# Routed rows scattered into one DRAM region per expert, tiles loaded plainly and turned on VectorE

## What is computed

```python
x = x + xattn(ctx_512, layernorm(x), Wq, Wk, gamma_raw)      # top-30% mask of similarities, made symmetric
h = layernorm(x).reshape(-1, 512)                            # 2048 tokens
scores = sigmoid(h @ router_w)                               # 2048 x 32
# 4 of 8 groups by their best two, then the best 8 experts in them
top_k_index = top_k(masked(scores + router_bias), 8)
tkw = 2.5 * scores[top_k_index] / sum(scores[top_k_index])
xs = repeat(h, 8)[argsort(top_k_index)]                      # 16384 rows, sorted by expert
down = ragged_dot(silu(ragged_dot(xs, w_gate)) * ragged_dot(xs, w_up), w_down)   # 512 -> 256 -> 512
shared = silu(h @ sw_gate) * (h @ sw_up) @ sw_down           # 512 -> 512 -> 512
x = x + sum_of_8(down * tkw) + shared
```

## Time and profile before

| | |
|---|---|
| median of 3 runs | 1012.5 us |
| profiled execution | 1009.42 us |
| its span, first to last instruction | 1007.7 us |
| PE (TensorE) busy | 905.1 us, 90% |
| DVE (VectorE) busy | 576.2 us, 57% |
| ACT (ScalarE) busy | 501.0 us, 50% |
| POOL (GpSimd) busy | 448.7 us, 45% |
| first matmul of the first expert tile | at 311.61 us |
| row transposes (L1490) | 592, on 148 tiles |

### The profile page before, as it was taken

The page is one execution under the profiler, slowest core; times in us unless marked ns, Lnnn a source line. Parts: engine busy times, 40 slices in busy tenths (PEclk is TensorE's granted clock), DMA queues, the critical chain, the costliest instruction groups (busy, mean ns, idle before and its releaser), DMA issues.

```text
span 1007.7 us, 21989 instructions
## 1 busy us (share of the span) xinstructions
PE 905.1 (90%) x4596; PEld 489.2 (49%) x4597; DVE 576.2 (57%) x1285; ACT 501.0 (50%) x994; POOL 448.7 (45%) x348
## 2 busy tenths in 40 slices
PE   4358798897969999999999999999999999999994
PEld 1143354544534555555555555555555555555542
DVE  5868798897886443446353455444455555463321
ACT  4376482752224444456454464545556455464331
POOL 1131011110033566555656665646465564566653
PEclk8569878898879999999999999999999999999998
DMA  4122021111228678878878888887788888787864
GB/s 155 42 80 80 1 85 54 43 46 42 93 84 270 155 177 191 184 170 222 185 168 192 180 186 196 169 221 171 175 219 204 234 187 235 174 187 127 147 114 77
DMA packets 90268, 149.25 MB, mean 148 GB/s; under 512 B 9649, under 2 KB 46769, under 8 KB 90225
## 3 DMA queue, kind: packets, MB, share of 16 engines
q0 software_dynamic: 33120, 80.64, 40.3%
q1 hardware_dynamic: 57104, 68.13, 21.2%
HBM read 101.55 MB, written 47.20 MB: 148 GB/s over the span
## 4 chain that ended last, share of the span: by engine, by line
PE 58%; issue 4%; DVE 3%; ACTq 2%; ACT 2%; DVEq 2%; POOL 0%; POOLq 0%
PE bank L258 49%; PE bank L1490 5%; PE bank L1481 3%; ACTq L1158 1%; ACT gu L240 1%; DVEq L1158 1%; DVE hid L1391 1%; DVE gu L247 1%; DVE mark_p L400 0%; DVE mark_q L407 0%; DVE dn L250 0%; ACTq L240 0%; DVEq L247 0%; DVE hid L309 0%; POOL out_dram L1201 0%
## 5 line engine op out<-in xcount | busy, mean ns | idle before, releaser
L258 PE MATMUL bank<-gu,xgT 128*128 x1764 | 404.8, 379 | 1.4 <-issue 1.4
L1201 POOL DMA_INDIRECT out_dram<-y,ids_i x145 | 236.4, 1630 | 233.3 <-DMA out_dram<-y,ids_i 120.5
L1383 DVE TENSOR_TENSOR xgT<-bank,xgT 128x512 f16<-128x512 f32 x148 | 102.2, 691 | 283.2 <-ACT xgT L1244 233.8
L258 PEld LDWEIGHTS bank<-gu,xgT 128*128 128x128 f16 x1764 | 172.4, 98 | 176.9 <-issue 1.6
L258 PE MATMUL bank<-dn,hT 128*128 x870 | 211.7, 379 | 0.8
L1189 POOL DMA_INDIRECT xg<-xrows,ids_i x153 | 167.0, 1092 | 68.3 <-issue 42.4
L1244 ACT CAST xgT<-bank 128x512 f16<-128x512 f32 x148 | 86.9, 588 | 135.6 <-issue 128.5
L1269 ACT ACTIVATE y<-bank 128x512 f32<-128x512 f32 x145 | 87.2, 601 | 110.1 <-PE bank L258 93.0
L258 PEld LDWEIGHTS bank<-dn,hT 128*128 128x128 f16 x870 | 84.9, 98 | 75.3 <-issue 7.8
L1250 ACT ACTIVATE silu<-bank 128x256 f32<-128x256 f32 x147 | 56.1, 382 | 97.7 <-PE bank L258 85.4
L1391 DVE SCALAR_TENSOR_TENSOR hid<-bank,xg,silu 128x256 f32<-128x256 f32 x147 | 70.6, 480 | 59.1 <-ACT silu L1250 52.7
(11 more groups left out here) (217 smaller groups left out, 793.4 us busy)
## 6 DMA issues: line engine op xcount, KB each, us to landing
stage_gu<-in_L_ffn_w_gate_dram SPq DMA_DIRECT2D x32, 512.0 KB
stage_gu<-in_L_ffn_w_up_dram SPq DMA_DIRECT2D x32, 512.0 KB
stage_dn<-in_L_ffn_w_down_dram SPq DMA_DIRECT2D x32, 512.0 KB
x_sb<-in_x_dram SPq DMA_DIRECT2D x4, 1024.0 KB, 6.7
xrows<-adj SPq DMA_DIRECT2D x4, 1024.0 KB, 4.2
out_dram<-acc SPq DMA_DIRECT2D x4, 1024.0 KB, 4.6
xg<-xrows,ids_i POOLq DMA_INDIRECT x153
out_dram<-y,ids_i POOLq DMA_INDIRECT x145
```

The source lines that it names most:

```text
L258: last = nc.tensor.matmul(out_ap, stationary(a, c), moving(w, c), start=(c == 0 and (a, w) == parts[0]), stop=(c == chunks - 1 and (a, w) ...
L1201: g_.indirect_dma_start(out, bass.IndirectOffsetOnAxis(ap=ids_i[:, t:t + 1], axis=0), y[:, t % YS, :], None, compute_op=ALU.add).then_inc( ...
L1383: v.tensor_tensor(xgT[:, s, 1, :, :], bank[XB[s]][:, :].rearrange("p (k t) -> p k t", k=KC), xgT[:, s, 0, :, :], ALU.subtract).then_inc(S[ ...
```

## The change

`xrows` and its gather are gone. A DRAM tensor `places` holds for each expert 16 x 128 row places, and 32 tiles more for rows that don't count. At routing each row goes to the place that its slot names: one indirect DMA for 128 tokens and one of their 8 choices (`dispatch_rows`), 32 for a batch and 128 in all, on GpSimd's queue. 24 of a batch stand in the first block in the pass behind its keys, 8 in the next pass between `s_low` 1 and 2; of batch 2 the last 8, and all 32 of batch 3, stand in the second block. The rest of each expert's last tile is filled with zeros by one more such DMA per expert (`fill_up`). Tiles are then read by SP with plain loads, five per tile (`load_rows`): four 128-column pieces, each onto 32 partitions in runs of 512 bytes, and the shares in runs of 128 bytes. VectorE turns a tile in 32x32 blocks with one instruction (`turn_rows`), whose result has the order of hidden values p * 4 + k; the weights of gate and up are loaded in the same order, which gives runs of 4 KB. SP's loop now goes over tiles. The row splits read SBUF instead of PSUM. `acc` and `xT16` keep fewer batches.

```diff
+        places = nc.dram_tensor("places", [E * TT + E, P, HR], F32).ap()
...
+        def dispatch_rows(pool, b, n):
+
+            k, i = TOP_EXPERTS - 1 - n // RT, n % RT
+            nc.gpsimd.indirect_dma_start(places.rearrange("t p h -> (t p) h"), bass.IndirectOffsetOnAxis(ap=slot[:, b % 2, i, k:k + 1], axis=0),
+                                         rows[:, b % 2, i, :], None).then_inc(S[f"dispatched{b}" if b < B - 1 else f"last{k}"], 16)
...
+                base(0)
+                for b in range(B):
                     if b >= 1:
-                        for c in range(SC):
-                            s_low(pool, b - 1, c)
+                        s_low(pool, b - 1, 0)
+                        s_low(pool, b - 1, 1)
+                    if b >= 2:
+                        for n in range(FIRST, RT * TOP_EXPERTS):
+                            dispatch_rows(pool, b - 2, n)
+                    if b >= 1:
+                        s_low(pool, b - 1, 2)
+                        s_low(pool, b - 1, 3)
+                    if b + 1 < B:
+                        base(b + 1)
+                    if b >= 1:
+                        pool.wait_ge(S["keys_ready"], b)
+                        pool.wait_ge(S["routed"], b)
+                        for n in range(FIRST):
+                            dispatch_rows(pool, b - 1, n)
...
+                def load_rows(t, x, at):
+
+                    tile = places[bass.ds(at, 1)].rearrange("t p h -> (t p) h")
+                    for q in range(RT):
+                        sp.dma_start(xq[q * 32:(q + 1) * 32, x, :, :],
+                                     tile[:, q * P:(q + 1) * P].rearrange("(g r) h -> r g h", r=32)).then_inc(S[f"gathered{x}"], 16)
+                    sp.dma_start(share_of[:, x, :], tile[:, H:]).then_inc(S[f"gathered{x}"], 16)
+
+                sp.wait_ge(S["places_ready"], 1)
+                for b in range(B - 1):
+                    sp.wait_ge(S[f"dispatched{b}"], 16 * RT * TOP_EXPERTS)
+                for t in range(XG):
+                    sp.wait_ge(S[f"last{TOP_EXPERTS - 1 - t}"], 16 * RT)
+                    sp.wait_ge(S[f"filled{t}"], 16)
+                    load_rows(t, t, info_of(sp, 4, t))
...
+                def step(t, ahead, x):
+                    at = info_of(sp, 4, t + ahead)
+                    sp.wait_ge(S["tile_hid"], t + (ahead - XG + 1))
+                    load_rows(t + ahead, x, at)
+                    next_load(t)
...
+                g_.memset(zero_row[:, :], 0.0).then_inc(S["zero_ready"], 1)
+                for n in range(FIRST, RT * TOP_EXPERTS):
+                    dispatch_rows(pool, b - 1, n)
+                pool.wait_ge(S["keys_ready"], b + 1)
+                pool.wait_ge(S["routed"], b + 1)
+                for k in range(TOP_EXPERTS):
+                    for i in range(RT):
+                        dispatch_rows(pool, b, k * RT + i)
+                    pool.wait_ge(S["fills_listed"], 1)
+                    pool.wait_ge(S["zero_ready"], 1)
+                    fill_up(k)
+                    if k in (0, 1, 3, 4):
+                        s_low(pool, b, (0, 1, None, 2, 3)[k])
...
+                def turn_rows(t, s, x):
+                    dve.wait_ge(S[f"gathered{x}"], (t - x) * (16 * PARTS // XG) + 16 * PARTS)
+                    if not (isinstance(t, int) and t < 2):
+                        dve.wait_ge(S["rows_low"], t - 1)
+                    v.transpose(xT[:, s, :, :].rearrange("p c (g r) -> p g c r", g=RT),
+                                xq[:, x, :, :].rearrange("p g (a c) -> p g c a", c=KC)).then_inc(S["rows_turned"], 1)
...
+                    turn_rows(t + 3, 1 - s, (x + 3) % XG)
                     split_rows(t + 2, s)
                     next_weights(fresh, e)
                     gates(t + 1, 1 - s, (x + 1) % XG, next_e)
...
-                def rows_T(t, s, x):
-
-                    pe.wait_ge(S[f"gathered{x}"], (t - x) * (16 // XG) + 16)
-                    if not (isinstance(t, int) and t < 2):
-                        pe.wait_ge(S["rows_low"], t - 1)
-                    for c in range(KC):
-                        last = nc.tensor.transpose(bank[XB[s]][:, c * P:(c + 1) * P], xg[:, x, c * P:(c + 1) * P], ident[:, :])
-                    last.then_inc(S["rowsT_ready"], 1)
```

More of the change, by code:

```diff
@@ L626, in rows_T @@
                         for k in range(KC):
[L627 removed]
+                            t = nc.tensor.transpose(bank[TB[i % 2]][:, k * P:(k + 1) * P], rows[:, b % 2, i, k * P:(k + 1) * P], ident[:, :])
                         t.then_inc(S["xnT_ready"], 1)
@@ L1133, in xattn_moe_kernel @@
         full = sb("full", [P, B])
+        odd = sb("odd", [P, B])
+        odd_full = sb("odd_full", [P, B], I32)
+        ends = sb("ends", [E, 1])
+        spare = sb("spare", [E, 1])
+        place = sb("place", [1, NT])
+        fill_at = sb("fill_at", [P, E])
+        fill_end = sb("fill_end", [P, E])
+        fill_row = sb("fill_row", [P, E])
+        fill_i = sb("fill_i", [P, E], I32)
+        fills = sb("fills", [P, E], I32)
+        zero_row = sb("zero_row", [P, HR])
         st = sb("st", [P, 1])
@@ new lines, in _, with next_load @@
+                sp.wait_ge(S["added"], TT)
+                sp.dma_start(out[(B - 1) * N:B * N, :].rearrange("(i p) h -> p i h", p=P),
+                             acc[:, (B - 1) % 3 * RT:(B - 1) % 3 * RT + RT, :]).then_inc(S[f"out_stored{B - 1}"], 16)
+                sp.wait_ge(S["tables_ready"], 1)
+                def next_load(t):
+                    with sp.If(info_of(sp, 5, t) > 0):
+                        at = tile_info[0:1, 0, t:t + 1] if isinstance(t, int) else tile_info[0:1, 0, bass.ds(t, 1)]
+                        e = sp.value_load(at, min_val=0, max_val=E - AHEAD - 3)
+                        n = e + (SH + AHEAD + 2)
+                        load(sp, n, n % 2, *(w[bass.ds(e + (AHEAD + 2), 1)].rearrange("a k n -> (a k) n") for w in (w_gate, w_up, w_down)))
@@ new lines, in step @@
+                def step(t, ahead, x):
[3 more added lines that the diff above has]
+                    next_load(t)
+                for t in range(E - XG):
+                    sp.wait_ge(S[f"filled{t + XG}"], 16)
+                    step(t, XG, t % XG)
+                with sp.Fori(E - XG, PLAIN - XG - 1, XG) as t:
+                    for i in range(XG):
+                        step(t + i, XG, i)
@@ L1173, in _ @@
+                next_load(PLAIN - 2)
+                next_load(PLAIN - 1)
+                for group in range(PLAIN, LEAST + E, SKIP):
+                    with sp.If(info_of(sp, 2, group) > 0):
+                        for t in range(group, min(group + SKIP, LEAST + E - 3)):
+                            with sp.If(info_of(sp, 2, t) > 0):
+                                step(t, XG - 2, (t + XG - 2) % XG)
             @block.gpsimd
@@ L1202, in scatter @@
                                           compute_op=ALU.add).then_inc(S[f"rows_added{t % YS}"], 16)
-                for t in range(XG):
-                    gather(t)
                 pool.wait_ge(S["tables_ready"], 1)
-                pool.wait_ge(S["out_stored"], 16 * B)
+                for b in range(B):
+                    pool.wait_ge(S[f"out_stored{b}"], 16)
                 for t in range(PLAIN - 1):
-                    gather(t + XG)
+                    if t + XG < E:
+                        fill_up(t + XG)
                     scatter(t)
@@ L1220, in _ @@
                     pool.wait_ge(S[f"rows_added{s}"], landed[s])
+                for x in range(XG):
+                    pool.wait_ge(S[f"gathered{x}"], arrived[x])
             @block.scalar
@@ L1321, in find_slots @@
                     ch.step(v.tensor_copy(st[:, :], bank[IDS][:, 0:1]))
-                    for j in range(2):
-                        ch.done(v.tensor_scalar(target[:, j * B:(j + 1) * B], full[:, :], st[:, 0:1], float(j), ALU.add, ALU.add))
+                    ch.step(v.tensor_scalar(full[:, :], full[:, :], st[:, 0:1], None, ALU.add))
+                    ch.done(v.tensor_tensor(target[:, 0:B], full[:, :], odd[:, :], ALU.add))
+                    ch.done(v.scalar_tensor_tensor(target[:, B:2 * B], full[:, :], 1.0, odd[:, :], ALU.add, ALU.subtract))
+                    ch.step(v.tensor_tensor(ends[:, :], st[0:E, :], tiles[:, :], ALU.add))
+                    ch.done(v.tensor_scalar(spare[:, :], tiles[:, :], -1.0, float(TT), ALU.mult, ALU.add))
+                    ch.done(v.tensor_scalar(steps[:, 2, :], tile_nof[0:E, :], ends[:, 0:1], None, ALU.is_ge))
                     ch.done(v.tensor_scalar(steps[:, 0, :], tile_nof[0:E, :], st[0:E, 0:1], None, ALU.is_ge))
```

211 lines of the change are left out of this document (119 added, 92 removed).

## The result

The changed kernel takes 1207.7 us (median of 4 runs, 1201.6 to 1216.0) against 1013.8 (4 runs, 1011.9 to 1016.0): ratio 1.192, 95% interval 1.184 to 1.200. I had forecast 1032, in a range of 985 to 1080. The sign was right, and the size was wrong by 176 us.

The account below looks back on a forecast made before the run. TensorE was taken to bound the expert stage, VectorE and a join the front. 1009.4 us profiled + 47 front loss - 27 stage gain = 1029.4; the median 3.1 above gives 1032.5, called 1032. Range 985 to 1080.

Parts of the forecast that it names:

- SyncE's queue: Expert stage: SyncE's loads and register reads need 4.3 us per tile against a mean pitch of 4.48, covered by eight buffers.
- rival C: Expert stage gains nothing because SyncE's five loads or the transfers set the pitch at 4.66 us: 1060 us, chance 0.12.
- The stage's gain: Expert stage: removed row transposes save 64 us, 37 come back as stalls, leaving 27 us gained.
- The stalls at the conversions: Expert stage: TensorE waits for VectorE's chain where weights are converted, 1.22 us more for each of some 30 experts, 37 us.
- The turn's price: VectorE, expert stage: one 128x512 f32 turn per tile costs 0.70 us, between bounds of 0.48 and 1.38.
- Scatter's price: GpSimd, ahead of the experts: each of the 128 indirect DMAs takes p = 1.4 us.
- Rival B: Front scatters on GpSimd cost what scatter-adds cost, 1.93 us each: 1088 us, chance 0.11.
- A: Rival: front scatters stay at 1.26 us and the expert stage's conversions find slack: 982 us, chance 0.27.
- After the join: Front: the last low half comes 51.5 us after the join, delaying the shared down product by 26.1 us.
- The 2 us that I added for the clock: Front: TensorE's idle time costs clock, 2 us of the 47 us lost there.
- The join: Front: GpSimd's scatters delay the join of all engines, 7.5 us through batches 1 and 2 and 11.8 through the last 24.
- Transfers: Expert stage: smaller packets cost about the same, 0.95 us per tile against 1.0; the share rises from 0.82 to some 0.86.

Follow-up runs that it names:

- e24: The changed kernel with each new expert's three weight loads always taken from one expert's weights at a constant address: 1161.5 us.
- e1: The changed kernel with each tile's rows fetched by one plain DMA instead of four, values wrong: 1090.3 us.
- e17: The changed kernel with one plain row DMA per tile from a fixed place of the input and no scatters of batches 0 to 2: 1033.3 us.
- e3: The changed kernel with the last batch's four low halves of the shared hidden tile moved ahead on GpSimd: 1215.2 us.
- e21: The changed kernel with each of the 96 scatters of batches 0 to 2 replaced by two GpSimd memsets, tile rows from a fixed place: 1110.0 us.
- e7: The changed kernel with the 96 scatters of batches 0 to 2 carrying 32 floats per row instead of 544, tile rows from a fixed place: 1130.0 us.
- e2: The changed kernel with SyncE's loop body holding 16 tiles instead of 8: 1191.4 us.
- e14: The kernel before the change with TensorE's loop over the 128 expert tiles written out as straight code: 1019.7 us.
- e19: The changed kernel with two GpSimd memsets behind each of the first 24 scatters of batches 0, 1 and 2, to spread them: 1272.1 us.

## Why the prediction was wrong

1. **SyncE's queue: the step that failed.** I costed it at 4.3 us a tile and called it "covered, narrowly". It is 5.5 (73 tiles in 400 us). Its parts: the tile alone 4.5 (3.95 by my terms: 5 x 0.55 + 1.2), weights (6.94 - 4.5) / 4.3 = 0.6 (I had 0.38, issues only), the loop's edge (8.12 - 4.5) / 8 = 0.45, which I did not have. Within the tile the five issues were right, 729.30 - 726.56 = 2.74 us against 2.75; the register reads, with the branch that I left out, take 731.06 - 729.30 = 1.76 against 1.2. Behind the edge is, as far as the packets show, code loading, worth 46 us in e24. Two unlike sums a few per cent apart (4.3 against 4.48) decide nothing; that was a case for most of the chances, and rival C had 0.12.
2. **Rival C had the mechanism and a false floor.** It let the stage "gain nothing" at a pitch of 4.66. A queue has no reason to stop there: its 5.5 became the pitch. With e1's load the stage loses 117 us less.
3. **The stage's gain, 27 us forecast.** e17 shows none beyond the error: 3 us won by the medians, 7 lost by the profiled executions. The stalls at the conversions were about right: TensorE's waits in e17 are 24.5 us in 400, 2.5 before, and 20 experts begin in 400 us, so 1.1 each where I had 1.22. Missing were two losses. One is in the ordinary tile: e17's busy time is 92.82 x 20 / 438 = 4.24 us per tile, and its products and transposes alone are 2.59 + 0.22 + 1.30 = 4.11. The same surplus before the change was smaller, 99.04 x 24 / 519 = 4.58 against 4.54, so some 0.09 us a tile or 13 us in all are new; no run says why. The other is the start of the stage, 2.9 tiles fewer in 169 us or some 13 us, where SyncE waits for zero fills, which I had costed for the first eight tiles only. The turn's price was mis-sized, 1.108 us against 0.70, and cost 7 to 9 us. The Trainium skill's figure (VectorE: DVE Perf Modes, The three transpose paths) had given 1.24 by my estimate, nearer to the measured 1.108.
4. **Scatter's price: right.** 1105 ns + 0.30 = 1.41 on the mean, p = 1.4. Rival B was wrong, and so was A's condition.
5. **After the join: right.** The last low half ends 366.0 - 315.2 = 50.8 us behind it (51.5 forecast). It was not worth anything as long as SyncE set the end (e3). The 2 us that I added for the clock come from no row, and no run shows them.
6. **The join: 291 forecast, 315.2 measured.** I summed GpSimd's own time, and e21 confirms that part (+18, I had 7.5 + 11.8); the last 24 scatters took 34.2 us, 33.6 forecast. What I left out is what its DMAs do beyond that (25 us): the last batch starts 17 us late behind ScalarE's late releases, and 7 us more lie between the last scatter and the join. I wrote "TensorE has nothing to do meanwhile"; it had, at under a third of its speed in after, but e7 shows that this did not set the join.
7. **Transfers: not the bound, as forecast.** The share of 0.86 belonged to a shorter pitch; it fell to 0.74 with the longer one.

From 1013.8 to 1207.7: front 69 (43 the join, 25 the low half, 1 rest), stage 123, of which e1 gives back 113 (its stage is 706.4 us): SyncE's queue.

## What to carry to other kernels

When a change moves work to a queue, sum that queue's whole period as if it were an engine: issues, register reads, branches, rarer branches by their frequency, and the edge of its loop; and look whether the loop's code still fits, for which the packets of the instruction queue beside a long tile at the edge are the sign. Here the measured period was 28% over the sum (5.5 against 4.3), and the sum had stood 4% under the pitch. A sum that close is to be measured, or price the case in which it sets the pitch without a floor. A join can come later than the last work of every engine on its list: compare kernels with and without the suspect before naming the engine that is slow ahead of it. A saving on the bound engine counts only up to the length of the next chain: here 46 us taken off TensorE were worth 15.

## What the runs showed of the hardware

- 128 x 512 f32 turned in 32x32 blocks on VectorE: 1.108 us.
- A SyncE DMA is issued every 0.50 us from a register address, 0.45 from a constant one (4 in 1.83 and 1.74 us with the last one's end); two register reads with their branch take 1.76 us between a tile's last DMA and the next one's first.
- SyncE's loop of eight tiles with register addresses in all its DMAs: 45 instruction packets against 7 to 9 in 400 us for the kernels with fewer of them, and 46 us over 14 turns (e24). The price is at the edge: with 7 edges instead of 14 there are 38 packets and 16 us less (e2).
- Written out as straight code, TensorE's 128 tiles show on another instruction queue, q8: 49 packets in the whole run against 14, with q14 unchanged (29 against 30), and no time lost that a single run can tell (e14).
- 24 indirect DMAs of 128 rows 1.27 us apart give ScalarE 50 us of late releases in 170 us and TensorE gaps of 7 to 15 us; 32 floats per row do it as 544 do (36 and 9 us), and 2.5 us apart they do not (e19).
- A join of the engines comes 7.51 us behind GpSimd's last indirect DMA in ten kernels, and 0.41 us behind its last memset in e21.
